# Second operands of the message stage in PSUM, the old sum ahead of the product, and the first maximum ahead of the one-hot rows

## The reference

```
scores = leaky_relu(e_s[edge_src] + e_d[edge_dst], 0.2)
m      = segment_max(scores, edge_dst)
ex     = exp(scores - m[edge_dst])
denom  = segment_sum(ex, edge_dst)
msg    = alpha[:, :, None] * h[edge_src]       # alpha = ex / denom[edge_dst]
agg    = segment_sum(msg, edge_dst)            # 2500 nodes x 256
```

## Time and profile before

| | us |
|---|---|
| median of 3 runs | 2734.74 |
| lowest and highest | 2731.53, 2736.45 |
| the profiled execution, its own time | 2739.28 |
| the span that its trace covers | 2737.2 |
| stretch of the messages, layer one | 361 to 1060 |
| stretch of the scores, layer two | 1449 to 1752 |
| stretch of the messages, layer two | 1885 to 2452 |

### The profile page before, as it was taken

One profiled execution on the slowest core, in us unless ns is written; L12 is line 12 of the kernel. 1 busy time (PEld: TensorE's weight loads), 2 busy tenths in 40 slices (PEclk: granted clock), 3 DMA queues, 4 the chain that ended last, 5 costly groups with the idle time before them and its releaser, 6 DMA issues. The chain is left out here.

```text
span 2737.2 us, 36321 instructions
## 1 busy us (share of the span) xinstructions
PE 1815.5 (66%) x10655; PEld 1474.6 (54%) x10655; DVE 1752.0 (64%) x2694; ACT 573.9 (21%) x1106; POOL 1643.0 (60%) x1456
## 2 busy tenths in 40 slices
PE   2795046777655554999886777405677777757688
PEld 1674034555444443699875555403555555546577
DVE  6689335777544447455675666796567777758675
ACT  2463100000000002354412222203000000004454
POOL 3477777887877773100007777788888888850050
PEclk8797567888877776799989999857788889878899
DMA  3266544554333333000023666733454444440010
GB/s 139 58 214 204 178 120 147 167 159 157 105 92 93 92 92 96 1 1 0 18 79 105 213 213 218 244 98 103 152 162 159 158 159 154 132 118 9 5 43 31
DMA packets 118702, 320.73 MB, mean 117 GB/s; under 512 B 37113, under 2 KB 63121, under 8 KB 104811
## 3 DMA queue, kind: packets, MB, share of 16 engines
q0 software_dynamic: 62272, 170.01, 21.9%
q1 hardware_dynamic: 55754, 145.31, 15.1%
q10 hardware_dynamic: 608, 4.59, 0.4%
HBM read 248.70 MB, written 71.12 MB: 117 GB/s over the span
## 5 line engine op out<-in xcount | busy, mean ns | idle before, releaser
L800 POOL DMA_INDIRECT e_ring<-table,e_index x840 | 1081.5, 1288 | 257.6 <-issue 256.1
L1187 PE MATMUL ms_ps_m<-ms_msg,ms_pick 128*128 128x260 f32 (+1 forms) x2816 | 859.7, 474 | 480.3 <-issue 266.5
L1187 PEld LDWEIGHTS ms_ps_m<-ms_msg,ms_pick 128*128 128x128 f32 x2816 | 659.0, 239 | 680.9 <-issue 532.8
L839 POOL DMA_INDIRECT e_ring<-table,e_stage_index x416 | 422.1, 1015 | 125.9 <-issue 120.9
L1164 DVE TENSOR_TENSOR ms_msg<-e_ring,all_xn 128x1040 f32 x176 | 217.8, 1237 | 354.0 <-SPq L1128 354.0
L690 PE MATMUL sc_ps_e<-sc_keys,sc_hot 125*128 125x100 bf16 (+1 forms) x3840 | 280.9, 229 | 86.8 <-DVE all_xn L643 86.5
L690 PEld LDWEIGHTS sc_ps_e<-sc_keys,sc_hot 125*128 125x128 bf16 x3840 | 254.7, 98 | 136.7 <-DVE all_xn L643 109.4
L1164 DVE TENSOR_TENSOR ms_msg<-e_ring,e_weight 128x1056 f32 x176 | 220.6, 1253 | 168.1 <-SPq L1128 168.0
L1160 DVE SCALAR_TENSOR_TENSOR ms_pick<-graph_dst_col,graph_tile_base,graph_lane_row 128x512 f32<-128x512 f32 x352 | 263.1, 748 | 11.4 <-issue 9.8
L605 ACT ACTIVATE sc_rows<-sc_ps_b 125x512 bf16<-125x512 f32 x320 | 173.0, 596 | 322.8 <-PE sc_ps_b L678 321.2
L643 DVE TENSOR_REDUCE all_xn<-sc_ps_e 128x800 f32 (+1 forms) x240 | 229.1, 982 | 1.4 <-PE sc_ps_e L690 1.3
(11 more groups left out here) (421 smaller groups left out, 2668.6 us busy)
## 6 DMA issues: line engine op xcount, KB each, us to landing
ahead<-e_ring SPq DMA_DIRECT2D x32, 1056.0 KB, 4.4
e_ring<-ahead SPq DMA_DIRECT2D x32, 1056.0 KB, 5.0
ahead<-e_ring SPq DMA_DIRECT2D x20, 1040.0 KB, 4.5
e_ring<-ahead SPq DMA_DIRECT2D x20, 1040.0 KB, 5.0
e_ring<-table,e_index POOLq DMA_INDIRECT x840, 2.8
e_ring<-table,e_stage_index POOLq DMA_INDIRECT x416
w_w<-L_ffn_w SPq DMA_DIRECT2D x2, 2048.0 KB
table<-qkv_v SPq DMA_DIRECT2D x5, 528.0 KB
```

The lines of the kernel that those rows point to most:

```text
L800: pool.indirect_dma_start(out=g.ring[:, slot * QUAD + i // GT, i % GT, :], out_offset=None, in_=s.table[:, :], in_offset=bass.IndirectOffs ...
L839: pool.indirect_dma_start(out=stage.rows[:, b, t, :], out_offset=None, in_=s.table[:, :], in_offset=bass.IndirectOffsetOnAxis(ap=stage.ind ...
L1187: mm = pe.matmul(ps_m[b][:, 0:W], pick[:, b, t, :], msg[:, b, t, :], start=t == 0, stop=t == GT - 1)
```

## The change

It has three parts.

1. In the message stage the second operand of two DVE instructions moves from SBUF to PSUM. ACT copies `lane_row` once to a PSUM bank (`ps_lane`), and `pick` reads it there. The weights go to PSUM too (`ps_w`): in layer one all 2560 values at once, in one ACT copy; in layer two 32 values for every step, by a new ACT copy ahead of the one that was there, and DVE waits for it (`weight_set`). To have the banks free, `ps_m` goes from three buffers to two, and PE waits for the sum of two steps ago in place of three.
2. In a step, DVE adds the old sum (of step n-2) ahead of the product in place of behind it.
3. In the scores, DVE takes the first maximum of item i ahead of the one-hot rows of item i+2, and the last one behind them. In layer one, which has one maximum an item, the order stays as it was. Nothing is moved on POOL's or SP's queue.

```diff
+            def turn_item(it, q, more=True):
+                for sub in range(SUBS - 1):
+                    select(it, q, sub)
+                if more:
+                    one_hot(it + HOTS, (q + HOTS) % lanes, False)
+                select(it, q, SUBS - 1)
-            with steps_of(dve, lanes, NITEM, lanes) as it0:
-                for q in range(lanes):
-                    one_hot(it0 + q, q, False)
-                    select(it0 + (q - 2), (q - 2) % lanes)
+            with steps_of(dve, 0, NITEM - lanes, lanes) as it0:
+                for q in range(lanes):
+                    turn_item(it0 + q, q)
...
-        ps_m = [m.ps(f"ps_m{i}", [P, 512]) for i in range(DEPTH)]
+        BANKS = 2
+        ps_m = [m.ps(f"ps_m{i}", [P, 512]) for i in range(BANKS)]
+        ps_lane = m.ps("ps_lane", [P, 512])
+        lane_row = ps_lane[:, 0:P]
+        ps_w = m.ps("ps_w", [P, ET, H]) if most is None else [m.ps(f"ps_w{i}", [P, 512]) for i in range(DEPTH)]
...
                 if later(fixed, DEPTH):
                     act.wait_ge(summed, n - (DEPTH - 1))
+                act.activation(ps_w[b][:, 0:GT * H].rearrange("p (t h) -> p t h", h=H), weight[:, bass.ds(group * GT, GT), :], ACT.Copy).then_inc(weight_set, 1)
                 act.activation(msg[:, b, :, R:W], most[:, bass.ds(group * GT, GT), :], ACT.Copy).then_inc(tail_ready, 1)
-            if most is not None:
+            act.wait_ge(between.back_copied, backs)
+            act.activation(lane_row, s.lane_row[:, :], ACT.Copy).then_inc(near_set, 1)
+            if most is None:
+                act.activation(ps_w[:, :, :], weight[:, :, :], ACT.Copy).then_inc(weight_set, 1)
+            else:
                 act.wait_ge(most_kept, 1)
                 staged(act, iteration, NS)
...
                     dve.scalar_tensor_tensor(out=pick[:, b, :, :], in0=s.dst_col[:, bass.ds(group * GT, GT)].unsqueeze(2).broadcast_to([P, GT, P]),
-                                             scalar=s.tile_base[:, bass.ds(tile, 1)], in1=s.lane_row[:, :].unsqueeze(1).broadcast_to([P, GT, P]),
+                                             scalar=s.tile_base[:, bass.ds(tile, 1)], in1=lane_row.unsqueeze(1).broadcast_to([P, GT, P]),
                                              op0=ALU.subtract, op1=ALU.is_equal).then_inc(pick_ready, 1)
-                    dve.wait_ge(rows_landed, group + 1)
-                    dve.tensor_tensor(msg[:, b, :, 0:R].rearrange("p t (h o) -> p t h o", h=H),
-                                      ring[:, bass.ds(slot, 1), :, :].rearrange("p a t (h o) -> p (a t) h o", h=H),
-                                      weight[:, bass.ds(group * GT, GT), :].unsqueeze(3).broadcast_to([P, GT, H, O + 1]), ALU.mult).then_inc(msg_ready, 1)
                 if later(fixed, LATE):
                     dve.wait_ge(summed, n - (LATE - 1))
...
-                    dve.tensor_tensor(into, into, ps_m[(b - LATE) % DEPTH][:, 0:W], ALU.add).then_inc(added, 1)
+                    dve.tensor_tensor(into, into, ps_m[(q - LATE) % BANKS][:, 0:W], ALU.add).then_inc(added, 1)
+                if fixed is None or fixed < NS:
+                    dve.wait_ge(rows_landed, group + 1)
+                    if most is None:
+                        shares = ps_w[:, bass.ds(group * GT, GT), :]
+                    else:
+                        dve.wait_ge(weight_set, n + 1)
+                        shares = ps_w[b][:, 0:GT * H].rearrange("p (t h) -> p t h", h=H)
+                    dve.tensor_tensor(msg[:, b, :, 0:R].rearrange("p t (h o) -> p t h o", h=H),
+                                      ring[:, bass.ds(slot, 1), :, :].rearrange("p a t (h o) -> p (a t) h o", h=H),
+                                      shares.unsqueeze(3).broadcast_to([P, GT, H, O + 1]), ALU.mult).then_inc(msg_ready, 1)
...
-                if later(fixed, DEPTH):
-                    pe.wait_ge(added, n - (DEPTH - 1))
+                if later(fixed, BANKS):
+                    pe.wait_ge(added, n - (BANKS - 1))
```

More of the change, by code:

```diff
@@ L637, in one_hot, with select @@
                 dve.tensor_scalar(hot[0:KEYS, q % HOTS, :], rows[0:KEYS, q, :], s.node_of[0:KEYS, 0:1], None, ALU.is_equal).then_inc(hot_ready, 1)
[L639 to L643 removed]
+            def select(it, q, sub):
+                dve.wait_ge(looked, it * SUBS + (sub + 1))
+                found = ps_e[(q * SUBS + sub) % BANKS][:, :].rearrange("p (t c) -> p t c", c=SLOT)[:, :, 0:C].rearrange("p t (g h) -> p t h g", h=H)
+                dve.tensor_reduce(edge[:, bass.ds(it * ITEM + sub * SL, SL), :], found, AX.X, ALU.max).then_inc(picked, 1)
+            def turn_item(it, q, more=True):
[4 more added lines that the diff above has]
+                select(it, q, SUBS - 1)
             dve.memset(pair[:, :, :, :], 0.0).then_inc(pair_zero, 1)
@@ L659, in _ @@
                 dve.tensor_copy(keys[0:LOW, :, his, :], found).then_inc(keys_ready, 1)
-            for q in range(lanes):
-                one_hot(q, q, True)
-                if q >= 2:
-                    select(q - 2, q - 2)
-            with steps_of(dve, lanes, NITEM, lanes) as it0:
-                for q in range(lanes):
-                    one_hot(it0 + q, q, False)
-                    select(it0 + (q - 2), (q - 2) % lanes)
-            for it in range(NITEM - 2, NITEM):
-                select(it, it % lanes)
+            for q in range(HOTS):
+                one_hot(q, q, True)
+            with steps_of(dve, 0, NITEM - lanes, lanes) as it0:
+                for q in range(lanes):
+                    turn_item(it0 + q, q)
+            for q in range(lanes):
+                turn_item(NITEM - lanes + q, q, q + HOTS < lanes)
         @block.tensor
@@ L1085, in staged @@
             for n in range(first):
-                iteration(n, n % DEPTH, n)
+                iteration(n, n, n)
             with eng.Fori(0, (NS - first) // unroll) as turn:
                 for q in range(unroll):
-                    iteration(turn * unroll + (first + q), (first + q) % DEPTH, None)
+                    iteration(turn * unroll + (first + q), first + q, None)
             for n in range(NS, last):
-                iteration(n, n % DEPTH, n)
+                iteration(n, n, n)
         def later(fixed, than):
@@ L1137, in _, with iteration @@
         def _(act):
-            def iteration(n, b, fixed):
+            def iteration(n, q, fixed):
+                b = q % DEPTH
                 (group,) = step_values(ENG.Activation, n, slice(2, 3), (NG - 1,))
@@ L1154, in _, with iteration @@
             dve.wait_ge(acc_zero, 1)
-            def iteration(n, b, fixed):
+            dve.wait_ge(near_set, 1)
+            if most is None:
+                dve.wait_ge(weight_set, 1)
+            def iteration(n, q, fixed):
+                b = q % DEPTH
                 slot, tile, group, tile_late = step_values(ENG.DVE, n, slice(0, 4), (RING - 1, NT - 1, NG - 1, NT - 1))
@@ L1183, in iteration @@
                     pe.wait_ge(tail_ready, n + 1)
-                if later(fixed, DEPTH):
-                    pe.wait_ge(added, n - (DEPTH - 1))
+                if later(fixed, BANKS):
+                    pe.wait_ge(added, n - (BANKS - 1))
                 for t in range(GT):
-                    mm = pe.matmul(ps_m[b][:, 0:W], pick[:, b, t, :], msg[:, b, t, :], start=t == 0, stop=t == GT - 1)
+                    mm = pe.matmul(ps_m[q % BANKS][:, 0:W], pick[:, b, t, :], msg[:, b, t, :], start=t == 0, stop=t == GT - 1)
                 mm.then_inc(summed, 1)
```

7 lines of the change are left out of this document (2 added, 5 removed).

## The result

| | before | after |
|---|---|---|
| median, us | 2733.82 | 2505.06 |
| lowest and highest | 2731.53, 2736.45 | 2504.01, 2509.46 |
| profiled execution: own time, span | 2739.28, 2737.2 | 2504.01, 2502.2 |

The median before is that of four executions now, where 2734.74 was that of three. The ratio is 0.9165 (95% interval 0.9152 to 0.9178), a gain of 229 us. The forecast was 2495, in a range of 2480 to 2560.

What follows compares the result with a forecast made beforehand. POOL's unbroken row of gathers was taken to bound both message stages. Savings of 112.1 and 127.4 us (239.5) from 2739.28 gave 2499.8; that execution being 4.5 above the median, the forecast was 2495 us, range 2480 to 2560.

Steps and rivals of the forecast that it cites:

- POOL's row sets the end: Both message stages: POOL's gathers and 0.30 us gaps fill 686 of 699 us and 565 of 567 us.
- the second SBUF operand stretches it: Message stages: gathers starting inside product or `pick` stand still, ending 0.82 us behind; freed, they take 0.950 us.
- Messages one, 112.1 us: Layer one's messages: 458 gathers fall from 547.2 us to 0.950 us each, so 112.1 us go.
- PSUM operands at no cost: Product and `pick` in a step: PSUM source adds zero; rival of slow PSUM, 2790 us, chance 0.06.
- new bound in the ahead turns: Rival in turns with ahead gathers: DVE or low-clock PE becomes slowest, 2525 us (2510 to 2560), chance 0.11.
- the ring: Message stages: 16 groups deep, some 40 us before a DVE lag stops POOL; nothing taken for it.
- Layer two, 127.4 us: Layer two's messages: 340 gathers at 0.950 us save 137.2 us, less 9.8 for one long gather: 127.4.
- part 3 at zero: Layer two's scores: 84 us earlier for PE, DVE and ACT, but POOL's 256 ahead gathers cover it: zero.
- 50.6: Layer two: excess in us above 0.950 each of 289 gathers, the ahead ones and turn 0, before the change.
- harmless instructions: DVE instructions taken not to hold gathers, which average 0.950 us beside the scores; memset and PSUM maxima were named.
- Items of 2.7 us, first product near 1845: Layer two: score items fall from 3.79 to 2.7 us; first product near 1845 against 1885.5 before.
- 40 us: Layer two: 40 of the 50.6 us stretch expected on the ahead gathers, putting the first product near 1845.

Runs made afterwards that it cites:

- e12: The changed kernel with GpSimd pausing half way through each eight gathers until four have landed: 2837.71 us, against 2737.46 for the kernel before on that chip.
- e1: Kernel before plus part 1 alone (second operands in PSUM, product still ahead of the old sum): 3510.69 us, against 3360.47 before on that chip.
- e2: Kernel before plus part 2 alone (old sum ahead of the product, operands still in SBUF): 3372.47 us, against 3360.47 before on that chip.
- e6: e5 with the product's weights read from SBUF again: 3376.89 us, against 3361.73 for the kernel before on that chip.
- e7: e5 with `pick`'s row read from SBUF again: 3455.16 us, against 3361.73 for the kernel before on that chip.
- e5: Kernel before plus parts 1 and 2, the scores keeping their old order: 3506.27 us, against 3361.73 for the kernel before on that chip.
- e10: The changed kernel with the messages' loop written out for 12 steps instead of 6: 3446.32 us, against 3360.14 for the kernel before on that chip.
- e11: Kernel before plus parts 1 and 2, with layer two's last-edge marks read from PSUM: 3523.59 us, against 3360.14 for the kernel before on that chip.

## Why the prediction was right, and what it missed

**POOL's row sets the end; the second SBUF operand stretches it: right.** e12 shows the first, e1, e2, e6 and e7 the second, with the 0.82 us behind the holding instruction. "SBUF — State Buffer", "Who interferes with whom", of the Trainium skill says the same of two SBUF inputs, and e5 to e7 agree; its inference that `tensor_tensor` doesn't stall descriptor generation is contradicted by e6, where 156 gathers are long. What the section says of at most one SBUF input it says only of instructions outside the modes of VectorE that use two ports, and it lists `tensor_scalar` among those that can be in one. The prediction left this condition out, and the one-hot rows, below, are what it missed by that: they have one tensor in SBUF, and they hold gathers (40 of 55 after the change). In which mode they run no trace says; 490 ns for 1024 elements is less than half of the 1.04 ns an element that the prediction has for the product.

**Messages one, 112.1 us: 113.2 measured for the whole of layer one's edges.** The gathers take 0.947 us, not the 0.950 used; 458 × 0.003 is 1.4.

**PSUM operands at no cost: right**, with the repeated element. The product went from 1253 to 1259 ns and `pick` from 748 to 752. So "VectorE: DVE Perf Modes" of the skill, with 62 fixed cycles more for a PSUM source, isn't borne out by these rows.

**No new bound in the ahead turns: right.** POOL waited for DVE less than 1 us in each message stage. DVE's sums waited for PE more than before (55.0 us in 50 waits in all, against 7.7 in 11), now that the sum stands ahead of the product, and the ring took that up. No run tells part 2's share in this on a chip of the first kind.

**Layer two, 127.4 us: 117.8 measured. Here the step failed that put part 3 at zero** ("this covers all of it"). The cover was there, but the new order has a price that I gave to the weights alone. The 256 ahead gathers take 301.3 us, 58.1 above 0.950 each, where I had counted on 50.6 (their excess before and that of turn 0 together). The excess in gathers that start inside the one-hot rows rose from 0.6 us (68 gathers, none above 1.1 us) to 9.9 us (55, of which 40 are above 1.1); that in the rest fell by 1.8. Over the whole of layer two the 628 gathers take 653.7 us where the forecast comes to 774.5 − 127.4 = 647.1, which is 6.6 us; POOL's index copies take 10.6 us in place of 8.9 (one of them, 4.1 us long, is held); and the last sum ends 9.5 us behind the last gather in place of 8.3. 6.6 + 1.7 + 1.2 = 9.5 of the 9.6 us missing.

One item of the scores of layer two before, then after, shows how that comes:

```profile
1594.01 0.48 DVE L637 TENSOR_SCALAR sc_hot<-sc_rows,all_node_of 125x1024 bf16<-125x1024 bf16 x1 [1.50 <-PE sc_ps_e L690]
1594.33 0.97 POOL L839 DMA_INDIRECT e_ring<-table,e_stage_index  x1 [0.30 <-issue]
```

```profile
1539.92 0.49 DVE L637 TENSOR_SCALAR sc_hot<-sc_rows,all_node_of 125x1024 bf16<-125x1024 bf16 x1 [0.18 <-PE sc_ps_e L694]
1540.02 1.20 POOL L843 DMA_INDIRECT e_ring<-table,e_stage_index  x1 [0.30 <-issue]
1541.53 0.95 POOL L843 DMA_INDIRECT e_ring<-table,e_stage_index  x1 [0.30 <-issue]
1542.68 0.49 DVE L637 TENSOR_SCALAR sc_hot<-sc_rows,all_node_of 125x1024 bf16<-125x1024 bf16 x1 [0.26 <-PE sc_ps_e L694]
1542.79 1.20 POOL L843 DMA_INDIRECT e_ring<-table,e_stage_index  x1 [0.30 <-issue]
```

The one-hot row is 0.49 us long, and almost every gather that starts in it ends 0.82 us behind it or later. Before, an item took 3.79 us, and three gathers at 1.25 (0.95 and the gap of 0.30) are 3.75. The gathers that met a one-hot row started 0.32 us or more inside it (66 of 68), where 0.95 us reaches to that point or falls 0.03 short: the one shown is stretched to 0.97. Now an item takes 2.76 us, two gathers are 2.50, and the first of the two starts 0.10 us inside, ends at 1541.22 (0.81 behind 1540.41) and is held for 0.25 us. The hold brings the pair to the item's own period, so it happens again in the next. What it costs an item is what is missing between the two periods: 0.04 us before, 0.26 us now. In e12, which has the same scores, it was 65 of 71 gathers and 16.0 us. I had counted `L637` among the harmless instructions by the mean of 0.950 in the earlier trace rows, and that mean was one of phase.

The trace of before shows as much, in the scores of layer one, which I hadn't read for it: 13 of the 35 gathers that start inside a one-hot row there are above 1.1 us. One of them:

```profile
225.04 0.49 DVE L637 TENSOR_SCALAR sc_hot<-sc_rows,all_node_of 125x1024 bf16<-125x1024 bf16 x1
225.16 1.18 POOL L839 DMA_INDIRECT e_ring<-table,e_stage_index  x1 [0.30 <-issue]
```

It ends 0.81 us behind the one-hot row.

**Items of 2.7 us, first product near 1845: 2.76 us, and 1868.7.** The first product came at 1751.92, and 1868.7 is that on the clock of before (layer two started 116.8 us earlier). DVE was ready 61 us before:

```profile
1751.92 1.25 DVE L1197 TENSOR_TENSOR ms_msg<-e_ring,ms_ps_w 128x1056 f32<-128x1056 f32 x1 [61.24 <-SPq L1138]
```

The ahead gathers ended 55.7 us later by that clock (301.3 − 249.6 = 51.7, and 4.0 more of index copies among them), not 40 us: the long gather of the earlier trace rows is now among them, and so are the 9.3 us of the one-hot rows. The first product came 15.9 us behind them, where I had allowed 8.

**The number.** 10.1 us missing from 2495: the profiled execution of after took 2504.0 for 2499.8 (4.2 us; layer two's 9.6 less the 1.1 of layer one and the 4.0 outside, within 0.3), and it was 1.1 us below its median, not 4.5 above. That offset is 5.6 us, and 0.3 is the rounding to 2495: one execution's distance from the median doesn't carry over to another kernel. That the result lies so near the forecast is in part luck: the 4.0 us outside the layers of edges were in no term, and without them it would have been 2509.

## What stays open

Why the same kernel takes 3360 us on three chips, and 2734 and 2737 us in the result and in e12, and why on those three the other engines' instructions start late while POOL gathers. Each chip was used once, so it isn't shown either that the chip makes the difference, and not something else that differed between those times. By e10 it isn't the loop's turns. That gathers are what delays them is suggested by the two windows of e2 and by the order of e5, e7 and e6 (3506, 3455 and 3377 us, with 0, 24 and 113 us of holds in layer one), but e12, which was to add pauses there, ran on the other kind of chip. What each part costs or brings on a chip of the first kind was read from traces, not timed alone. Nor was e11's kernel run there; by the traces it would lose the long gather and the one-hot rows' holds, some 19 us less than the 2505, and that is an estimate.

## What to carry to other kernels

Where GpSimd's descriptor work is one unbroken row, look in the timeline for gathers that end a fixed time behind a VectorE instruction; putting the second operand of two such instructions into PSUM took some 240 us of holds away, for ScalarE copies of 0.2 us. A speed-up of a stage that is covered isn't free if its shorter period falls into step with the covering row: compare the periods, not the means. And time a change on more than one chip: this one brings 8.4% on one and costs 2.6% on another, where POOL's row doesn't set the end.

## What the runs showed that was not expected

**A hold through two instructions.** The 10.79 us gather of the earlier trace rows came again, and this time the load of 2.5 MB was issued only some 58 us later:

```profile
1680.05 10.79 POOL L843 DMA_INDIRECT e_ring<-table,e_stage_index  x1 [0.30 <-issue]
1680.09 4.59 DVE L1167 MEMSET all_acc<- 128x5440 f32 x1 [13.67 <-ACT ms_ps_lane L1157]
1684.60 5.43 DVE L1169 TENSOR_TENSOR e_dst_line<-e_dst_line,graph_is_last 128x5120 f32<-128x5120 f32 x1
```

It began 0.04 us ahead of a memset, which holds nobody in layer one, and ended 0.81 us behind the product that follows the memset. e12 has the same (10.78 us). So the hold of the product, which has two SBUF operands, seems to have reached back over the memset; how, no run shows.

**A start within the first 0.1 us may go free.** In e7 the gather at 707.54 starts with the `pick` and takes 0.95 us. In the scores of layer one before, all nine that start 0.06 us or less inside a one-hot row do so. After the change six of layer two that start 0.09 to 0.10 us inside one do too, while others with the same distance are held.

**The same code, two bounds.** In the window 130:330, in scores whose code is the same, PE did 1792 matmuls on one chip and 83 on another, with 0.59 and 0.65 of the DMA time in use.
